# First layer of a cross-attention block: queries and keys projected once, eight heads a time, and placed in doubled rows by way of DRAM

## What is computed

```
q = Wq x + bq ; k = Wk kv + bk ; v = Wv kv + bv         # 256 x 256 weights, per batch
attn = softmax(q^T k / sqrt(16), masked)                 # 16 heads, 512 x 512
mean = attn v ; ex2 = attn v^2 ; std = sqrt(relu(ex2 - mean^2))
xn = instance norm of x over the positions
out = (xn * std + mean) * mask
```

## Time and profile before

| what | value |
|---|---|
| median of three runs | 1786.55 us |
| span of the profiled execution | 1788.6 us |
| time around its span | the profile gives none |
| TensorE, VectorE, ScalarE, GpSimd busy | 96%, 75%, 61%, 20% |
| first layer, first to last scores | 16.05 to 644.8 us (first and last start of L392) |
| DMA moved over the span | 105.16 MB, mean 59 GB/s |

### The profile page before, as it was taken

The page is one execution under the profiler, slowest core; times in us unless marked ns, Lnnn a source line. Parts: engine busy times, 40 slices in busy tenths (PEclk is TensorE's granted clock), DMA queues, the critical chain, the costliest instruction groups (busy, mean ns, idle before and its releaser), DMA issues.

```text
span 1788.6 us, 33022 instructions
## 1 busy us (share of the span) xinstructions
PE 1711.6 (96%) x11812; PEld 1157.8 (65%) x11812; DVE 1342.2 (75%) x2857; ACT 1099.9 (61%) x2416; POOL 349.9 (20%) x435
## 2 busy tenths in 40 slices
PE   8999999999999998899989989999999899999999
PEld 4443333343433344788878777788878788888888
DVE  5778898888888766899998999999999873232222
ACT  3667676776767666777777877777778742121111
POOL 0002131221212141322232222232223130000000
PEclk9999999999999998999999999999999899999999
DMA  3101010110100033222223524333333340000000
GB/s 111 37 16 51 15 51 26 40 50 16 50 17 26 18 123 86 71 73 72 72 70 98 138 55 119 89 90 93 95 89 82 99 123 7 5 20 9 16 20 16
DMA packets 75297, 105.16 MB, mean 59 GB/s; under 512 B 21248, under 2 KB 36480, under 8 KB 75008
## 3 DMA queue, kind: packets, MB, share of 16 engines
q1 hardware_dynamic: 63552, 77.88, 15.3%
q0 software_dynamic: 9472, 20.99, 4.6%
q10 hardware_dynamic: 2112, 4.19, 0.8%
HBM read 39.55 MB, written 4.72 MB: 25 GB/s over the span
## 4 chain that ended last, share of the span: by engine, by line
PE 61%; DVE 23%; issue 7%; ACT 6%; SPq 2%; DMA 2%; POOL 1%; ACTq 0%; DVEq 0%; POOLq 0%
PE ps L419 11%; PE ps L1858 9%; PE ps L392 7%; PE ps L1832 7%; PE ps L365 5%; PE ps L1182 4%; DVE at_t L1311 4%; DVE at_t L1316 4%; PE ps L1192 3%; PE ps L1131 2%; PE ps L404 2%; PE ps L1837 2%; DVE nmax L510 2%; PE ps L1120 1%; ACT at_prob L1530 1%
## 5 line engine op out<-in xcount | busy, mean ns | idle before, releaser
L510 DVE TENSOR_REDUCE nmax<-ps 128x2 f32<-128x1024 f32 x256 | 311.2, 1220 | 97.2 <-PE ps L392 96.0
L687 ACT ACTIVATE prob<-ps 128x1024 f32<-128x1024 f32 x256 | 261.8, 1023 | 160.4 <-PE ps L404 159.1
L1530 ACT ACTIVATE at_prob<-at_t,at_nmax 128x256 f32<-128x256 f32 x512 | 256.4, 505 | 109.5 <-DVE at_nmax L1316 94.2
L419 PE MATMUL ps<-prob,v 128*64 128x512 f32 x1024 | 276.2, 618 | 0.0
L1316 DVE CUSTOM_DVE_ANT_0 at_t<-at_t,at_off 128x256 f32<-128x256 f32 x512 | 232.8, 491 | 8.9
L2017 DVE CAST mlp_h_hi<-mlp_h 128x512 fp32r<-128x512 f32 x64 | 29.5, 461 | 212.8 <-ACT mlp_h L1929 179.9
L1676 POOL TENSOR_TENSOR at_low<-at_low,at_high 128x512 fp32r<-128x512 f32 x64 | 86.2, 1346 | 480.2 <-DVE at_high L1345 480.1
L1929 ACT ACTIVATE mlp_h<-ps,b 128x512 f32<-128x512 f32 x48 | 33.1, 690 | 218.3 <-PE ps L1832 218.3
L1131 PE MATMUL ps<-ident,at_prob 128*128 128x128 f32 x1024 | 158.3, 277 | 0.0
L1120 PE MATMUL ps<-at_k_stack,at_q_stack 96*128 96x256 f32 x512 | 119.0, 315 | 24.7 <-ACT at_prob L1530 22.3
L1311 DVE SCALAR_TENSOR_TENSOR at_t<-ps,mask_self 128x512 f32<-128x512 f32 x192 | 131.0, 682 | 10.2 <-PE ps L1120 10.1
(11 more groups left out here) (227 smaller groups left out, 4258.5 us busy)
## 6 DMA issues: line engine op xcount, KB each, us to landing
at_k_stack<-at_high SPq DMA_DIRECT2D x256, 64.0 KB, 2.4
at_q_stack<-at_high SPq DMA_DIRECT2D x128, 64.0 KB, 2.7
at_q_stack<-at_high POOLq DMA_DIRECT2D x128, 64.0 KB, 2.5
at_q_stack<-at_low SPq DMA_DIRECT2D x128, 64.0 KB, 2.1
at_k_stack<-at_low POOLq DMA_DIRECT2D x128, 64.0 KB, 2.3
c_in<-in_ctx SPq DMA_DIRECT2D x8, 512.0 KB, 3.6
X<-in_x SPq DMA_DIRECT2D x8, 512.0 KB, 4.8
mean_in<-v_out SPq DMA_DIRECT2D x128, 32.0 KB
```

The costliest lines, as they stand in the source:

```text
L419: mm = eng.matmul(ps[2 * QD * k:2 * QD * (k + 1), VB, :], v[:, c, HG * G + 2 * p + k, :], prob[:, M % PROBS, k, :], start=(c == 0), stop=( ...
L510: eng.tensor_reduce(nmax[:, n % 2, j, 2 * p:2 * p + 2], ps[:, at:at + 2, :], AX, ALU.max, negate=True).then_inc(s_max, 1)
L687: eng.activation(prob[:, M % PROBS, :, :], ps[:, ST:ST + 2, :], ACT.Exp).then_inc(s_exp, 1)
L1530: ins = eng.activation(prob[:, m % 2, i, :], t[:, p, i, :], ACT.Exp, scale=-1.0, bias=nmax[:, m % 4, i:i + 1], accum_out=z[:, T % 2, j, 2 ...
```

## The change

Weights are no longer doubled. One query item projects 128 plain channels, eight heads, which is a pair of groups (`PAIRS` = 16). ScalarE takes the high part and VectorE the rest, once each, into `shares_of`. SP writes them in doubled, 32-row form to a DRAM tensor `rows0` with four slots (six DMAs for a pair) and reads each group's q1, q2 or k1, k2 back into the ring (four DMAs for a pair). The ones of q2 are written to DRAM once at the start and the mask rows of k2 once a batch (`far_out`). Items q and k of a pair stand at steps 3, 4 and 6, 7 of every even group. The first factor 1/4 moves into the exponential. The splits of x and context for the next batch, and the masks, move from the third group of a batch to the second. The filler before group 0 has 26 matmuls in place of 9. The core of the diff:

```diff
-        if s in (0, 1, 3, 4) and w + 1 < GROUPS:
-            return [("k" if s > 2 else "q", w + 1, (s % 3,))]
+        if s in (3, 4, 6, 7) and w % 2 == 0 and w // 2 + 1 < PAIRS:
+            return [("q" if s < 5 else "k", w // 2 + 1, (s % 3,))]
...
-        if s == 6 and w == 0:
+        if s == 5 and w == 0:
             return [("v", 0, (0, 1))]
...
+        def far_out(b):
+            eng.wait_ge(s_far, b + 1)
+            if b:
+                for n in range(NG * (b - 1), NG * b):
+                    eng.wait_ge(s_ring["k"][n % RING], (n // RING + 1) * DMA)
+            eng.dma_start(d["rows0"][ROWS.index("k2")].rearrange("s p t -> p s t"),
+                          far[:][:, None, :].broadcast_to([P, RING, D])).then_inc(s_far_out, DMA)
+        def rows_out(name, m):
+            k, slots = "qk".index(name), slice(2 * m % RING, 2 * m % RING + 2)
+            eng.wait_ge(s_high[name], m + 1)
+            taken(eng, name, m)
...
+            if name == "k":
+                eng.wait_ge(s_far_out, DMA * (m // 2 + 1))
+            for n in range(2 * m - RING, 2 * m - RING + 2):
+                if n >= 0:
+                    eng.wait_ge(s_ring[name][n % RING], (n // RING + 1) * DMA)
+            for tensor, part, at in ((0, 0, 0), (1, 0, 0), (0, 1, HD0)) if name == "q" else ((0, 0, 0), (0, 0, HD0), (1, 1, 0)):
+                eng.dma_start(d["rows0"][2 * k + tensor, slots].rearrange("s (h r) t -> (s h) r t", r=QD)[:, at:at + HD0, :],
+                              shares_of[:, k, part, :].bitcast(F32)).then_inc(s_out[name], DMA)
+        def rows_in(name, n):
+            k = "qk".index(name)
+            eng.wait_ge(s_out[name], 3 * DMA * (n // 2 + 1))
+            if n >= RING:
+                eng.wait_ge(s_st, 8 * (n - RING) + 8)
+            eng.dma_start(ring[:, n % RING, 2 * k:2 * k + 2, :].bitcast(F32),
+                          d["rows0"][2 * k:2 * k + 2, n % RING].rearrange("a p t -> p a t"))\
+               .then_inc(s_ring[name][n % RING], DMA)
...
+        eng.wait_ge(s_one, 1)
+        eng.dma_start(d["rows0"][ROWS.index("q2")].rearrange("s p t -> p s t"),
+                      scrap[:][:, None, :].broadcast_to([P, RING, D])).then_inc(s_const, DMA)
+        far_out(0)
...
+        rows_out("k", 0)
+        rows_in("k", 0)
+        rows_out("q", 0)
+        rows_in("q", 0)
+        rows_in("k", 1)
+        rows_in("q", 1)
...
+            if w % NG == 2 and b + 2 < NB:
+                far_out(b + 2)
+            if w % 2 and ahead < PAIRS:
+                rows_out("k", ahead)
+                rows_in("q", 2 * ahead)
+                rows_in("k", 2 * ahead)
...
+            if w % 2 and ahead < PAIRS:
+                rows_in("q", 2 * ahead + 1)
+                rows_in("k", 2 * ahead + 1)
+            if w % 2 == 0 and ahead < PAIRS:
+                rows_out("q", ahead)
...
-        busy(9, SC, wide[:].rearrange("p j c -> p (j c)"))
+        busy(26, SC, wide[:].rearrange("p j c -> p (j c)"))
...
-                        eng.wait_ge(s_k1, w + 1)
-                        eng.wait_ge(s_k2, w + 1)
-                        eng.wait_ge(s_q1, w + 1)
-                        eng.wait_ge(s_q2, w + 1)
+                        landed(eng, w)
...
+        def rest_of(name, m):
+            k = "qk".index(name)
+            eng.wait_ge(s_high[name], m + 1)
+            eng.scalar_tensor_tensor(out=shares_of[:, k, 1, :], in0=bank_of(name, m), scalar=b0[:, k, m % 2:m % 2 + 1],
+                                     in1=shares_of[:, k, 0, :].bitcast(F32), op0=ALU.add, op1=ALU.subtract)\
+               .then_inc(evicted(name, m), 1)
...
+                if w % 2 == 0 and s == 5 and w // 2 + 1 < PAIRS:
+                    rest_of("q", w // 2 + 1)
+                if w % 2 and s == 0 and w // 2 + 1 < PAIRS:
+                    rest_of("k", w // 2 + 1)
+                if w == 1 and s in (2, 3):
+                    low_weights(s - 2)
+                if w % NG == 1 and w // NG + 1 < NB and s in (4, 5):
+                    low_x(w // NG + 1, s - 4)
+                if w % NG == 1 and w // NG + 1 < NB and s in (6, 7):
+                    low_context(w // NG + 1, s - 6)
...
+        def high_of(name, m):
+            k = "qk".index(name)
+            made(eng, name, m)
+            if m:
+                eng.wait_ge(s_out[name], 3 * DMA * m)
+            eng.activation(shares_of[:, k, 0, :], bank_of(name, m), ACT.Identity, bias=b0[:, k, m % 2:m % 2 + 1])\
+               .then_inc(s_high[name], 1)
...
+        eng.activation(scrap[:], wide[:].rearrange("p j c -> p (j c)").bitcast(F32), ACT.Identity,
+                       bias=row[:, ONE_AT:ONE_AT + 1]).then_inc(s_one, 1)
         masks(0)
-        high_k(0)
-        take_q(0)
-        second_q(0)
+        high_of("k", 0)
+        high_of("q", 0)
...
+                if w % 2 == 0 and s == 5 and w // 2 + 1 < PAIRS:
+                    high_of("q", w // 2 + 1)
+                if w % 2 and s == 0 and w // 2 + 1 < PAIRS:
+                    high_of("k", w // 2 + 1)
...
-                if s == 7 and w % NG == 2 and b + 1 < NB:
+                if s == 6 and w % NG == 1 and b + 1 < NB:
                     masks(b + 1)
...
-                if w % NG == NG - 2 and b + 1 < NB:
-                    if s == 3:
+                if w % NG == 1 and b + 1 < NB:
+                    if s == 2:
                         high_x(b + 1)
-                    if s == 5:
+                    if s == 4:
                         high_context(b + 1)
```

More of the change, by code:

```diff
@@ L35 @@
 DMA = 16
-NEG_LO, IS_LOW, ONE_AT, FAR_AT, FAR_OFF = range(5)
+ONE_AT, FAR_AT, FAR_OFF = range(3)
+ROWS = ("q1", "q2", "k1", "k2")
 class Count:
@@ L85, in layer0 @@
     GROUPS = NB * NG
+    PAIRS = GROUPS // 2
     LAG = 12
@@ L172, in layer0 @@
         s_zero = sem("zero")
-        s_b0 = sem("b0")
+        s_const = sem("const")
+        s_one = sem("one")
+        s_far_out = sem("far_out")
+        s_out = {name: sem("rows_" + name) for name in "qk"}
+        s_ring = {name: [sem(f"ring_{name}{k}") for k in range(RING)] for name in "qk"}
         s_score = sem("score")
@@ L182, in layer0 @@
         s_free = sem("free")
[L183 to L186, removed]
+        s_high = {name: sem("high_" + name) for name in "qk"}
         s_sq = sem("squares")
@@ L231, in made, with landed @@
             eng.wait_ge(s_item, number[(name, n)] + 1)
+        def landed(eng, n):
+            for name in "qk":
+                eng.wait_ge(s_ring[name][n % RING], (n // RING + 1) * DMA)
         def regrouped(n, k):
@@ L310, in shares_out @@
                               .broadcast_to([NH // 2, HD0, D])).then_inc(s_rw, DMA)
-        for w in range(2, GROUPS + 3):
-            n, b = w - 2, w // NG - 1
+        for w in range(GROUPS + 3):
+            n, b, ahead = w - 2, w // NG - 1, w // 2 + 1
             if w % NG == 2 and b >= 0:
                 shares_in(b)
-            if n < GROUPS:
+            if 0 <= n < GROUPS:
                 regroup(2 * n)
@@ L341, in item @@
             bank = bank_of(name, n)
-            b, G = n // NG, n % NG
+            b, half = n // 2, n % 2
             if n == 0 and name == "v":
@@ L347, in item @@
             if name in "qk":
-                col = slice(P * G, P * (G + 1))
+                col = slice(P * half, P * (half + 1))
                 if b == 0:
-                    if G == 0 and 0 in parts:
+                    if half == 0 and 0 in parts:
                         eng.wait_ge(s_first_x if name == "q" else s_first_c, DMA)
@@ L545, in squares_of_x @@
         def squares_of_x(b, h):
+            if b == 0 and h == 0:
+                eng.wait_ge(s_const, DMA)
             eng.tensor_tensor_reduce(scrap[:], X[:, b, h, :], X[:, b, h, :], 1.0, 0.0,
@@ L695, in masks @@
             if b:
-                eng.wait_ge(s_k2, NG * b)
+                eng.wait_ge(s_far_out, DMA * b)
             eng.wait_ge(s_mask, b + 1)
@@ L2113, in build @@
         keep(ctx, "ident", [P, P])
-        keep(ctx, "row", [P, 5])
+        keep(ctx, "row", [P, 3])
         keep(ctx, "gb", [P, 3, 2, DC])
@@ L2193, in along_columns @@
         return np.broadcast_to(b, (P, b.shape[0]))
-    def twice(w):
-        w = w.reshape(w.shape[0], NH, 1, HD0)
-        return np.concatenate([w, w], 2).reshape(w.shape[0], D)
     where = np.arange(P) % QD
-    row = np.zeros((P, 5), np.float32)
-    row[:, NEG_LO] = np.where(where >= HD0, -1.0, 0.0)
-    row[:, IS_LOW] = np.where(where < HD0, 1.0, 0.0)
+    row = np.zeros((P, 3), np.float32)
     row[:, ONE_AT] = np.where(where == HD0, 1.0, 0.0)
```

160 lines of the change are left out of this document (51 added, 109 removed).

## The result

The changed kernel takes 1778.6 us (median of 6 runs, 1772.35 to 1781.13), beside 1789.26 for the kernel before on the same chip. The ratio is 0.993 with a 95% interval of [0.9914, 0.9946]: 10.7 us faster, where 24 were forecast. The median lies just inside the range of 1750 to 1779, at its end. The profiled execution is the fastest of the six: its span is 1770.6 us, and its run 1772.35.

The account below looks back on a forecast made before the run. TensorE was taken to bound the kernel, with the exponential chain holding empty intervals at 1.86 us. Terms -40.3 + 4.0 - 1.6 + 10.2 + 0.6 = -27.1, less 3 taken back, -24: 1763 us, range 1750 to 1779.

Parts of the forecast that it names:

- the head: Opening before the first scores: serial DRAM writes and reads on SP move scores from 16.05 to 26.2, 10.2 us more.
- the clock's term: Group 0: starting at a lowered TensorE clock after standing adds 0.6 us (0 to 2).
- The halves: Groups 3 to 30: 56 fewer projection halves on TensorE at 0.72 each save 40.3 us.
- the stalls: Groups 3 to 30: stalls total 23.9 us against 19.9 now, so 4.0 us is given back.
- allowance of 3: Whole kernel: 3 us taken back for collisions that could not be placed, half a microsecond a batch.
- The new stalls behind high x and high context: Second group of a batch: ScalarE's moved splits delay the exponential by about 0.9 and 0.8, 1.7 us a batch.
- VectorE's burst in that group: Second group, steps 4 to 7: 11.3 us of VectorE work, taken as costing nothing; up to 2 a batch if that fails.
- "Nothing" for the rows through DRAM: Odd-to-even group turns: the key's trip takes about 10 us with 6 to 7 us spare, so it costs nothing.
- rival B: Rows late at odd-to-even turns: 1838 for all 15 pairs, 1805 if only the 7 with the mask row; chance 0.08.
- Rival C: Opening: a dearer head, with hops at 5.5 adding 8 us and a low clock 2, gives 1773; chance 0.12.
- Groups 0 to 2: First three groups: 1.6 us saved by fewer halves, with 0.6 added for the clock.
- Rival A: Groups 3 to 30: ScalarE and VectorE stalls take most of the gain, net -7, 1780; chance 0.15.

Follow-up runs that it names:

- e3: Changed kernel with the three matmuls of each projection half in batches 1 to 7 issued twice; median 1814.07 us, ratio 1.0135 to the kernel before.
- e4: Changed kernel with high x moved to the first group of a batch and the context splits to the third; median 1772.73 us, ratio 0.9917.
- e6: Changed kernel with the edits of e2 and e4 together; median 1760.4 us, ratio 0.9839 to the kernel before.
- e2: Changed kernel with high and low parts in neighbouring DRAM rows, so a write goes to 128 places, not 8 blocks; median 1768.65 us, ratio 0.9887.
- e1: Changed kernel with 98 filler matmuls before group 0 in place of 26; median 1772.25 us, ratio 0.9902 to the kernel before.
- e8: e7 without the fifteen filler matmuls of steps 5 and 7 of group 0; median 1754.85 us, ratio 0.9803 to the kernel before.
- e9: The changed kernel once more, no edit; median 1777.16 us, ratio 0.9932 to the kernel before.
- e5: e2 with both sets of row writes in the opening issued before the first read; median 1766.22 us, ratio 0.9866 to the kernel before.
- e10: e5 with 60 filler matmuls before group 0 in place of 26; median 1764.25 us, ratio 0.986 to the kernel before.
- e7: e6 with e5's order, 38 fillers, and only two slots of the constant rows written ahead of the first reads; median 1750.29 us, ratio 0.9786.
- e11: e7 with 48 filler matmuls in place of 38; median 1750.72 us, ratio 0.9782 to the kernel before.

## Why the prediction was half right

The sign, the place of the gain and the main term were right; the size was off by 13 us of the median. The step that failed is the head, forecast at 10.2 and measured at 17.5; behind it stands the clock's term of 0.6.

1. **The halves (-40.3) and the stalls (+4.0): right.** Groups 3 to 30 took 521.4, and the sum without its allowance of 3 gives 523.7. The intervals are those forecast (2.57 and 1.88), and e3 shows TensorE on the path. That 0.72 was exactly the worth of a removed half is not shown: doubling costs 0.54 on average, and takes the place of waits that were there (some 0.5 us for maxima in the first group of a batch, gone in e3).
2. **The new stalls behind high x and high context: placed right, and of the size forecast.** ScalarE in the second group of a batch:

```profile
282.19 1.02 ACT L730 ACTIVATE prob<-ps 128x1024 f32<-128x1024 f32 x1 [0.82 <-PE ps L465]
284.01 0.60 ACT L758 ACTIVATE q2m<-ps 128x512 fp32r<-128x512 f32 x1 [0.80 <-PE ps L442]
284.51 1.05 ACT L770 ACTIVATE x_hi<-X 128x1024 fp32r<-128x1024 f32 x1
285.45 1.02 ACT L730 ACTIVATE prob<-ps 128x1024 f32<-128x1024 f32 x1
...
288.40 0.60 ACT L764 ACTIVATE v_out<-ps 128x512 f32<-128x512 f32 x1
288.90 1.05 ACT L775 ACTIVATE c_hi<-c_in 128x1024 fp32r<-128x1024 f32 x1
289.85 1.02 ACT L730 ACTIVATE prob<-ps 128x1024 f32<-128x1024 f32 x1
291.69 1.03 ACT L730 ACTIVATE prob<-ps 128x1024 f32<-128x1024 f32 x1 [0.83 <-PE ps L465]
```

   Where ScalarE only takes an exponential it waits 0.82 or 0.83 for TensorE: that is the slack of an empty interval, the 0.84 of the forecast. Behind the high parts it waits for nothing, so they end the interval. The intervals of TensorE there last 2.71 and 2.46 in place of 1.86: 1.45 a batch against 1.7. The moments' stall was 0.5, as forecast. VectorE's burst in that group, put at nothing, cost some 0.5 a batch: TensorE waits 0.53 to 0.58 for maxima at the start of the third group, and in e4 and e6 this wait is gone. Together 1.9, what the second group fell by in e4. Placed elsewhere the work costs something too: e6 gains 7.4 us over 28 groups on e2, 1.2 for each of the six batches that are split ahead.
3. **"Nothing" for the rows through DRAM: wrong by 2.5 to 5.** I reckoned with a key's trip that begins 2.7 into an odd group and takes 10, and called the rest of the 17 "6 to 7 us spare"; those numbers leave 4.3. The key's shares were ready 1.9 in (167.42), but SP, which works in order, issued regroups of values first; the trip begins 6.6 in (172.11 against 165.5) and takes 11.7, together 18.3, and nothing was spare. So rival B's mechanism, for which I gave a trip of 14.5 as the turning point, began below 12. The waits are 5.4 us at seven turns, mostly those of B's second form, with the mask rows ahead. Net they cost less: e2, which has none of them, took 2.5 less in groups 3 to 30, and waits 0.8 for the exponential at most of the same places. The allowance of 3 covered that.
4. **The head (+10.2): the step that failed.** It cost 17.5 to the scores and 18.0 to the maxima. All of the miss to the scores, 7.3, stands in two terms, the three 256 KB writes at 6.9 and 7.7 us for 3.3 and 4. I priced them by rows of loads and never asked on how many places the destination was laid out. e2 changes that alone and gets 3.3 and 5.8. So the layout accounts for 5.5 of the 7.3; the 1.8 left in the query's writes go together with the key's read, which shares the queue with them and which I had let run beside them at no cost (that it is the cause was not tested). The estimate that the prediction worked out from the Trainium skill, page "DMA: Bandwidth & Descriptors", section "Anatomy of one DMA" (scores near 27), missed by nearly as much, with bytes at the full rate too; that section is about DMAs issued from GpSimd, and these go out on SP. Rival C had the right place and nearly the size (8 for a miss of 7.3), with the wrong cause: hops, not the rate.
5. **Groups 0 to 2 (-1.0 with the clock): was +1.2 in the trace, and likely more in other executions.** TensorE stood 16.3 us where 5 to 6 were forecast (the 26 fillers ended at 17.3 and not at 20.5), and came back at half clock (0.56 over 33.6 to 45). The clock's term, 0.6 (0 to 2), is too small by the median: e1, which keeps TensorE at work, takes 6.3 off it. The fillers that I left "where they were" also meet the values:

```profile
45.56 2.12 PE L487 MATMUL ps<-ring 128*128 128x512 f32 x8
...
52.24 1.13 PE L416 MATMUL ps<-c_in,w 128*128 128x512 f32 x2 [1.92 <-DVE v L577]
...
54.03 3.35 PE L487 MATMUL ps<-ring 128*128 128x512 f32 x7
```

   The seven at 54.03 take 0.48 each, about twice the 0.25 of the 26 at full clock. e8, without both batches of fillers, was no faster.
6. **Rival A** (ScalarE and VectorE eat the gain) is refuted: groups 3 to 30 took 521.4, and its mark was over 535. Its price was added up wrongly: 38 us of stalls in place of 19.9 make the whole -13 and not -7, with groups 3 to 30 at 538.

**What stays open.** The profiled executions differ by 18.0, the medians by 10.7. The changed kernel's executions have spans from 1770.6 to 1779.3, and its profiled one was the fastest. e9, the same kernel, had a span of 1773.2 and a median of 1777.2. Over the thirteen traces the untouched part from group 31 on varied between 1155.6 and 1162.5, with the same instructions. Two things point at the clock for the rest. The mean granted clock of the profiled execution was 0.983, and that of the five others 0.980 or 0.981; e1's executions had 0.986 to 0.989. And the opening comes in two forms: the changed kernel and e9 were at half clock to 43.6 and then for 3.4 us, e3 and e4 to 52.3 and then for 6.8, which cost them 5 us in group 0. If the untraced executions of the changed kernel had the second form, that is the size of what e1 gained in the median beyond its trace. Only one execution of a set is traced, so this is not shown.

## What to carry to other kernels

When data goes by DRAM to be placed anew, price a write by its own layout and not by the rate of the loads: count how the outermost dimension of both sides divides, and look at the rate in the DMA view's slices. A hidden chain has a start, a length and a deadline, and the start must be read from the queue that issues it, with all that stands before it. Removing one stall can show less than it is worth while a second one ends at the same place; try the two together before dropping either. And one trace is one execution: see where it stands among the others before a difference of a few us is read from it.

## What the runs showed of the hardware that I had not expected

- Writes from SBUF to DRAM with 8 outer blocks moved some 200 GB/s, and those with 128 outer rows some 400, in packets of like size. The 16 DMA engines were busy some five tenths of the time in the first case and nine tenths in the second (e2).
- A clock once fallen stayed low while TensorE was busy. In its stand of 16.3 us the changed kernel's clock fell at 19.7, and it rose at 43.6, 10 us into steady work. In e5, whose TensorE stood 7.5 us, it was low just as long (19.7 to 43.6), and in e3 and e4, with the changed kernel's stand, for 30.7 us. In e10 it fell at 28.0, 3 us behind 60 fillers that ran without a gap into the scores, and stayed low for 13.7 us; e7 (a stand of 2.4) lost 13.7 us as well, and e11 (0.2) two pieces of 3.4 us. I can't say what tells e10 and e11 apart. The Trainium skill, page "TensorE: Matmul & The Clock Gate", part 1, says that throttled is the default and activity releases it; the stands of 16.3 and 7.5 us agree, and e10 shows that a low clock also comes without one.
